# First tiles of attention: masked keys made later, ScalarE's query copies and weight sums in another order

## What is computed

```python
q = x_q @ W_q.T + b_q
k = x_kv @ W_k.T + b_k
v = x_kv @ W_v.T + b_v
qh, kh, vh = (_split_heads(q), _split_heads(k), _split_heads(v))      # 16 heads of 16
scores = jnp.einsum('bhqd,bhkd->bhqk', qh, kh) * scale
attn = jax.nn.softmax(scores, axis=-1)
ctx = jnp.einsum('bhqk,bhkd->bhqd', attn, vh)
...
scale = 1.0 / jnp.clip(jnp.mean(jnp.abs(w)), 1e-05)                   # feed-forward weights
```

## Time and profile before

| | us |
|---|---|
| median of 3 runs | 682.3 (681.88 to 682.7) |
| the profiled execution | 682.72 |
| its span, first to last instruction | 680.9 |
| TensorE busy | 650.0 (95%) |
| VectorE busy | 613.7 (90%) |
| ScalarE busy | 384.4 (56%) |
| GpSimd busy | 365.1 (54%) |

### The profile page before, as it was taken

How to read it: one execution, slowest core, us unless ns; L and a number is a source line. 1 busy time by engine, 2 the same in 40 slices (tenths; PEclk the granted TensorE clock), 3 DMA queues, 4 the chain that set the end, 5 groups by cost and what they waited for, 6 DMA issues and landing times. The chain is left out here.

```text
span 680.9 us, 12450 instructions
## 1 busy us (share of the span) xinstructions
PE 650.0 (95%) x4268; PEld 477.6 (70%) x4284; DVE 613.7 (90%) x1241; ACT 384.4 (56%) x761; POOL 365.1 (54%) x506
## 2 busy tenths in 40 slices
PE   9999999999999999999999989888999999999996
PEld 3588765788747887568887677556777775666664
DVE  4899887999999999999999979867999979999997
ACT  4742158031358503575232633658888886888885
POOL 0633424537244753258451471654576669788786
PEclk9999999999999999999999999989999999999998
DMA  8730055231553446443753066643222221000112
GB/s 306 208 63 1 0 125 112 74 63 11 69 107 63 96 152 62 93 93 63 202 101 84 1 187 96 221 151 95 64 80 80 79 79 33 1 33 32 34 63 94
DMA packets 52680, 60.73 MB, mean 89 GB/s; under 512 B 5416, under 2 KB 46376, under 8 KB 52362
## 3 DMA queue, kind: packets, MB, share of 16 engines
q1 hardware_dynamic: 43498, 40.28, 18.3%
q0 software_dynamic: 8256, 18.86, 17.3%
q10 hardware_dynamic: 864, 0.79, 0.4%
HBM read 33.72 MB, written 11.53 MB: 66 GB/s over the span
## 5 line engine op out<-in xcount | busy, mean ns | idle before, releaser
L746 ACT ACTIVATE yb<-banks 128x256 f32<-128x256 f32 x64 | 24.2, 385 | 137.6 <-PE banks L445 92.4
L436 PE MATMUL banks<-inv_m,spec_y 128*128 128x256 f32 x384 | 85.5, 379 | 0.0
L472 PE MATMUL banks<-xt_in,w_in 128*128 128x512 f32 x192 | 84.5, 594 | 0.2
L436 PEld LDWEIGHTS banks<-inv_m,spec_y 128*128 128x128 f32 x384 | 73.0, 190 | 9.9
L388 PE MATMUL banks<-z_cplx,fwd_m 128*128 128x256 f32 x240 | 72.0, 381 | 3.6 <-DVE prod L1172 3.2
L389 PE MATMUL banks<-z_cplx,fwd_m 128*128 128x256 f32 x240 | 71.4, 379 | 0.0
L472 PEld LDWEIGHTS banks<-xt_in,w_in 128*128 128x128 f32 x192 | 36.1, 190 | 43.0 <-issue 40.2
L388 PEld LDWEIGHTS banks<-z_cplx,fwd_m 128*128 128x128 f32 x240 | 44.9, 190 | 11.9 <-issue 5.3
L389 PEld LDWEIGHTS banks<-z_cplx,fwd_m 128*128 128x128 f32 x240 | 45.6, 190 | 6.2
L904 POOL TENSOR_TENSOR spec_y<-prod 128x256 f32<-128x256 f32 x35 | 25.4, 727 | 42.0 <-DVE prod L1172 41.3
L2224 DVE TENSOR_REDUCE peak<-ps_score 128x16 f32<-128x1024 f32 x32 | 38.9, 1215 | 9.7 <-PE ps_score L1668 9.7
(11 more groups left out here) (311 smaller groups left out, 1706.2 us busy)
## 6 DMA issues: line engine op xcount, KB each, us to landing
x_tok<-in_x SPq DMA_DIRECT2D x8, 512.0 KB, 4.3
x_tok<-in_b_out POOLq DMA_DIRECT2D x8, 512.0 KB, 13.9
inv_scratch<-inv_sum SPq DMA_DIRECT2D x16, 256.0 KB, 2.6
xa_t<-inv_scratch SPq DMA_DIRECT2D x16, 256.0 KB, 2.7
v_t<-left POOLq DMA_DIRECT2D x8, 511.5 KB, 5.2
x_t<-left POOLq DMA_DIRECT2D x8, 511.5 KB, 5.6
xt_in<-in_x_t SPq DMA_DIRECT2D x3, 1024.0 KB, 5.9
x_scratch<-x_tok SPq DMA_DIRECT2D x6, 512.0 KB, 4.1
```

The source lines that it names most:

```text
L436: last = mm(bank[:, odd * 2 * P:(odd + 1) * 2 * P], spec_y[:, j + odd, part * D + h * P:part * D + (h + 1) * P], inv_m[:, o:o + 2 * P], st ...
L472: last = mm(proj_pair(b, t)[:, c * 512:(c + 1) * 512], w_in[:, k, TILES[t] * P:(TILES[t] + 1) * P], xt_in[:, k, c * 512:(c + 1) * 512], st ...
```

## The change

It moves three things and alters no instruction. VectorE makes `k_pairs` behind the second inverse in tile 6 instead of behind shift(1). TensorE does scores(3) between the two query halves of chunk 6 instead of behind both. ScalarE copies query halves one by one, with weight sums between them and in other places up to tile 8.

```diff
@@ TensorE @@
             query_half(Q_EARLY + 1, 0)
+            scores(3)
             query_half(Q_EARLY + 1, 1)
-            scores(3)
             turn_prob(2)
@@ ScalarE @@
-            evac_q(Q_EARLY + 1)
+            evac_q(Q_EARLY + 1, 0)
+            weight_sum(0, 0)
+            evac_q(Q_EARLY + 1, 1)
             exponentials(3)
             evac_prob(2)
             evac_x(Q_EARLY + 2)
             evac_prob(3)
             exponentials(4)
-            evac_q(Q_EARLY + 2)
-            weight_sum(0, 0)
+            evac_q(Q_EARLY + 2, 0)
+            weight_sum(0, 1)
+            evac_q(Q_EARLY + 2, 1)
+            exponentials(5)
+            weight_sum(1, 0)
             evac_prob(4)
             evac_context(0)
-            for j in range(5, TILES_ALL):
+            exponentials(6)
+            evac_context(1)
+            evac_prob(5)
+            weight_sum(1, 1)
+            evac_prob(6)
+            for j in range(7, TILES_ALL):
                 exponentials(j)
-                if j - 4 in range(6):
-                    weight_sum((j - 4) // 2, (j - 4) % 2)
+                if j < 9:
+                    weight_sum(2, j - 7)
@@ VectorE @@
-                if j == 1:
+                if j in (5, 6):
+                    invert(j - 5)
+                if j == 6:
                     for t in range(DT):
                         tt(k_pairs[:, t, 1:B], k_t[:, t, 1:B].unsqueeze(2).broadcast_to([P, B - 1, 2, NCTX]),
...
-                if j in (5, 6):
-                    invert(j - 5)
```

More of the change, by code:

```diff
@@ L1861, in evac_x, with evac_q @@
                     fn(x_t[:, c % 2, t, :], late_banks[t][:, :], ACT.Copy).then_inc(xt_evac, 1)
[L1863 to L1867, removed]
+            def evac_q(c, i):
+                t = late_order(c)[i]
+                act.wait_ge(q_mm, DT * (c - Q_EARLY) + i + 1)
+                fn(q_bufs[c // CHUNKS_B][:, t, c % CHUNKS_B * CH * P:(c % CHUNKS_B + 1) * CH * P], late_banks[t][:, :], ACT.Identity,
+                   bias=bq[:, t:t + 1]).then_inc(q_evac, 1)
             def weight_sum(i, h):
@@ L1942, in _ @@
             act.wait_ge(v_ready, 2 * B)
-            evac_q(Q_EARLY)
+            evac_q(Q_EARLY, 0)
+            evac_q(Q_EARLY, 1)
             evac_prob(0)
```

## The result

| | before | changed |
|---|---|---|
| median (5 runs each) | 682.7 us | 679.49 us (678.65 to 679.92) |
| ratio | | 0.9949 (0.9938 to 0.9961) |
| repeated (21 and 5 runs) | 682.49 us | 679.43 us, ratio 0.9950 (0.9937 to 0.9962) |
| profiled execution, span | 682.72, 680.9 | 679.56, 677.8 |
| start of scores(2), of scores(8) | 440.34, 470.96 | 441.36, 467.87 |

The kernel is faster by 3.1 to 3.2 us. The last three lines of the table say where. The changed stretch got 4.11 us shorter, and what follows it took the same time to 0.1 us. But the changed kernel reached scores(2) 1.02 us later, in code that is the same in both.

The account below looks back on a forecast made before the run. TensorE bounds attention's steady part; waits and a clock fall in its first tiles leave room. 1.80 + 1.67 + 0.86 = 4.33 us earlier scores(8) takes 682.72 to 678.39, less 0.42 to the median: 678.0, range 676.8 to 680.1.

Parts of the forecast that it names:

- Part 1: VectorE, `k_pairs` behind invert(1): shift(2) ends 1.96 us earlier; `k_pairs` takes 1.09 us (upper bound 2.98), costing nothing at either.
- Part 2: TensorE, scores(3) between chunk 6's query halves: transposing tile 3 starts at 449.75 instead of 451.55, 1.80 us gained.
- Part 3: TensorE from transposing tile 3 on: the wait shrinks, the clock no longer falls to half, 0.49 + 1.09 + 0.09 = 1.67 us gained.
- Part 4: ScalarE, no weight sum ahead of the copy of tile 5: transposing tile 6 comes 2.21 behind tile 5's, not 3.07; 0.86 us.
- k_pairs didn't meet GpSimd: Rival: behind invert(1), `k_pairs` blocked by GpSimd's multiply and addition; shift(7) and scores(8) 2.5 us back, 680.5; chance 0.04.
- nothing was given back behind scores(8): Rival: steady part or feed-forward is paced by something that doesn't move, so time stays at 682; chance 0.03.
- no long spell at half clock: Rival: TensorE drops to half clock in the short blocks of 447 to 470 and stays; slower, 683.7; chance 0.04.
- Rival 1: TensorE's clock falls again, by itself or in another stretch, taking back 1.67 us: 679.6; chance 0.13.

Follow-up runs that it names:

- keys_only: Kernel before with only `k_pairs` moved behind the second inverse, TensorE's and ScalarE's orders as before: 682.61 us, ratio 0.9998.
- keys_and_scores: Kernel before with `k_pairs` behind the second inverse and scores(3) between the query halves, ScalarE's order as before: 680.67 us, ratio 0.9969.
- scalar_only: Kernel before with only ScalarE's new order, `k_pairs` and scores(3) at their old places: 680.86 us, ratio 0.9978.
- filler: Kernel before with each of the eight transposes of x of chunk 7 done twice, nothing else: 681.74 us, ratio 0.9989.
- scores_only: Kernel before with only scores(3) moved between the query halves, `k_pairs` still behind shift(1): 680.80 us, ratio 0.9980.
- context_first: Changed kernel with evac_context(0) ahead of the copy of tile 4's weights on ScalarE: 678.45 us, ratio 0.9933 against the kernel before.
- keys_beside_gpsimd: Changed kernel with `k_pairs` behind shift(3), where GpSimd is adding the bias: 680.34 us, ratio 0.9987 against the kernel before.
- before_third: Kernel before, unedited, profiled once more: 681.85 us in one run, scores(2) to scores(8) 29.10 us.
- before_again: Kernel before, unedited, run again with its own profile: 682.82 us, ratio 1.0002.

## Why the prediction was right, and where its size was off

678.0 was forecast and 679.5 measured, inside the range of 676.8 to 680.1 and 1.5 above its centre.

**Part 1, right.** shift(2) ended 3.27 us behind the start of scores(2), forecast 3.28. `k_pairs` cost 0.96 where I took 1.09, and ended before multiply(0). The choice between its bounds was tested: beside GpSimd it is 3.19, so the lower bound was the right one for an idle GpSimd. That it is worth nothing by itself I had not said; keys_only shows it.

**Part 2, right.** scores(3) came 4.07 behind scores(2), forecast 3.97. Tile 3 came 1.72 earlier, forecast 1.80: a query half followed by scores takes 1.91 to the next start, not 1.82.

**Part 3, right in mechanism, wrong in two sizes.** The clock stayed full. In the trace the blocks from tile 3 to sums(0) took 5.46 instead of 6.99, so 1.53 and not 1.67. The 0.09 that I counted for the second query half was its length at full clock, and 1.82 should have been 1.91 in the middle term too. More serious is the step "it lies 0.42 above the median, so 678.0". It took the whole clock term over from one execution into the median. The fall is in about half of the executions of the kernel before, so its median holds only a part of the 1.52.

**Part 4, right.** 0.86 forecast, 0.86 measured (2.21 from tile 5 to tile 6, both times), and again as the difference between keys_and_scores and the changed kernel, and 0.87 in scalar_only.

**The sum.** 1.72 + 1.53 + 0.86 = 4.11 in the trace, forecast 4.33. The parts that are in every execution are 1.72 + 0.86 = 2.58, and the profiles without a fall agree: 29.10 less 26.51 is 2.59. The difference of the medians, 3.1 to 3.2, lies between 2.59 and 4.11, as it must if the fall is there in part of the executions. The other kernels fall into line: filler 0.4 (0 without the fall, 1.5 with), scores_only 1.4 (0.5 and 2.0), scalar_only 1.3 (0.9 and 2.4), keys_and_scores 1.8 (1.7 and 3.3), context_first 4.3 (3.4 and 4.9). Only keys_beside_gpsimd doesn't, with 1.8 (2.1 and 3.6), as four of its own ten executions have the mark of a fall. Taken by groups the medians fit better: the changed kernel (679.43) is 2.76 under the executions of the kernel before without the mark (682.19) and 3.76 under those with it (683.19), where the traces give 2.59 and 4.11.

The two groups of the kernel before are 0.8 to 1.2 apart, not 1.52. Why is open. The opening may give back the rest: three of the four profiled executions with the fall had a short one (7.03, 7.01, 6.84), and before_third without it a long one (8.04). But before_again had a long opening (8.09) and the fall, so the two don't always go together. What decides in one execution whether the clock falls is open as well.

The measured time lies within the range, but partly by luck. The upper end of 680.1 was there for a fall in the new order, and no such fall is what made the gain smaller. That the old order often runs without the fall stood in no rival.

**Rivals.** The clock didn't fall again, k_pairs didn't meet GpSimd, nothing was given back behind scores(8) (209.9 us in both), and no long spell at half clock came. Rival 1 gave nearly the measured time, 679.6, for the wrong reason.

## What to carry to other kernels

Where several engines take turns, an edit on one of them may be worth nothing alone (0.0 us) and still be worth 1.24 us with its partner. Follow the chain by hand to the next wait, on each engine, and test the parts alone. A stall that a trace shows once may not be in every execution; before a term of it goes into a median, take a second and a third profile of the same program, and read the mean clock of every timed execution. Put VectorE work on two operands in SBUF where GpSimd is idle.

## What the hardware showed that I had not expected

- The same program, with the same wait of 1.37 us on TensorE, dropped to half clock in some executions and not in others (30.62 and 29.10 us for the stretch), by the mean clock in about half of them.
- The six opening matmuls took 4.26 to 5.49 us in all, 592 to 1222 ns each, from one execution to the next; 1.2 us of difference before any work of the kernel proper.
- Two VectorE instructions on 128x384 took 0.96, 2.98 or 3.19 us by where GpSimd's additions lay, and GpSimd's additions took 0.6 longer in the last case. The Trainium skill ("SBUF — State Buffer", "Who interferes with whom") says that a VectorE instruction with two SBUF inputs contends with a GpSimd instruction that reads SBUF, and that the lock on the ports they share is exclusive. Here the first of the pair ran at its usual 549 ns and the other took 2728. That is 2.18 us more, nearly one addition of 2.36 us, and agrees.
